# Attention-and-experts kernel, prologue: K's second weights as one doubled transfer, two moved groups of splits, projection weights split in batch 0

## What is computed

```python
h = layernorm(x)                                   # (32, 112, 256)
q = (h @ Wq), k, v = ctx @ Wkv                     # 16 heads of 64
out = softmax(q k^T / 8) v                         # per head, 112 x 375
x = x + out @ Wproj + bproj
h = layernorm(x)
x = x + top-2-of-8 experts(h)                      # silu(h G) * (h U) @ D
```

## Time and profile before

| | |
|---|---|
| median of 3 runs | 1570.44 us |
| the profiled execution | 1568.5 us |
| its span, first to last instruction | 1566.4 us |
| TensorE matmul busy | 1503.0 us (96%) |
| VectorE, ScalarE, GpSimd busy | 968.7, 762.3, 555.2 us |

### The profile page before, as it was taken

How to read it: one execution, slowest core, us unless ns; L and a number is a source line. 1 busy time by engine, 2 the same in 40 slices (tenths; PEclk the granted TensorE clock), 3 DMA queues, 4 the chain that set the end, 5 groups by cost and what they waited for, 6 DMA issues and landing times. The chain is left out here.

```text
span 1566.4 us, 37570 instructions
## 1 busy us (share of the span) xinstructions
PE 1503.0 (96%) x12134; PEld 1321.0 (84%) x12135; DVE 968.7 (62%) x2579; ACT 762.3 (49%) x2091; POOL 555.2 (35%) x636
## 2 busy tenths in 40 slices
PE   4999999999999999999999999999996699999997
PEld 4888888898888888888888888898875588888886
DVE  5667677676766676767767676667675633333332
ACT  3555555555555555555555555555553322222221
POOL 5224233333433243423334343324355122323232
PEclk9999999999999999999999999999997799999999
DMA  5411111111112221111111111221016233332332
GB/s 152 131 50 50 56 49 55 49 55 50 54 54 60 64 73 54 49 54 49 54 49 57 49 54 54 65 69 52 12 66 227 52 52 51 50 54 47 53 50 28
DMA packets 82704, 96.19 MB, mean 61 GB/s; under 512 B 6912, under 2 KB 77808, under 8 KB 82672
## 3 DMA queue, kind: packets, MB, share of 16 engines
q1 hardware_dynamic: 68960, 74.67, 16.5%
q0 software_dynamic: 12144, 15.66, 6.2%
q10 hardware_dynamic: 1568, 5.44, 1.0%
HBM read 44.85 MB, written 50.90 MB: 61 GB/s over the span
## 5 line engine op out<-in xcount | busy, mean ns | idle before, releaser
L767 ACT ACTIVATE prob<-bank,neg_max 112x375 f32<-112x375 f32 x512 | 295.3, 586 | 138.1 <-DVE neg_max L1017 138.1
L1017 DVE TENSOR_REDUCE neg_max<-bank 112x1 f32<-112x375 f32 x512 | 243.9, 539 | 19.4 <-PE bank L1247 19.3
L1257 PE MATMUL bank<-ident,prob 112*125 112x112 f32 x1536 | 214.7, 274 | 2.6 <-ACT prob L767 2.4
L1257 PEld LDWEIGHTS bank<-ident,prob 112*125 112x125 f32 x1536 | 195.9, 188 | 13.8 <-ACT prob L767 4.9
L706 POOL DMA_INDIRECT out<-y_out,dest_now x63 | 97.8, 1552 | 244.1 <-ACT y_out L859 215.0
L895 DVE TENSOR_TENSOR K_l<-bank,K_h 128x376 fp32r<-128x376 f32 x256 | 140.4, 550 | 64.9 <-ACT K_h L727 62.4
L1281 PE MATMUL bank<-probT,V 125*64 125x112 f32 x3072 | 176.6, 264 | 2.0 <-DVE probT L1023 1.1
L1155 PE MATMUL bank<-Wgu,hT_h 128*128 x504 | 175.1, 429 | 2.9 <-DVE hT_l L1112 2.9
L1281 PEld LDWEIGHTS bank<-probT,V 125*64 125x64 f32 x3072 | 149.1, 137 | 14.6 <-issue 2.6
L885 DVE COPY V<-bank 125x512 f32<-125x512 f32 x96 | 66.4, 692 | 151.3 <-PE bank L1219 147.4
L1133 DVE COPY hidT<-bank 128x512 f32<-128x512 f32 x63 | 43.6, 692 | 173.7 <-PE bank L1462 173.7
(11 more groups left out here) (171 smaller groups left out, 3719.9 us busy)
## 6 DMA issues: line engine op xcount, KB each, us to landing
bins<-pad_rows SPq DMA_DIRECT2D x29, 1032.0 KB, 6.2
h_in<-bins SPq DMA_DIRECT2D x63, 129.0 KB, 2.2
y_sb<-in_ctx SPq DMA_DIRECT2D x32, 187.5 KB, 2.4
y_sb<-in_ctx SPq DMA_DIRECT2D x62, 93.8 KB, 2.5
Wgu<-in_L_ffn_gate_up_w SPq DMA_DIRECT2D x4, 1024.0 KB, 5.2
Wgu<-in_L_ffn_gate_up_w ACTq DMA_DIRECT2D x4, 1024.0 KB, 13.2
x_sb<-in_x SPq DMA_DIRECT2D x16, 224.0 KB, 2.8
x_res<-in_x SPq DMA_DIRECT2D x32, 112.0 KB, 5.6
```

Of the source, the lines that this page charges most:

```text
L767: nc.scalar.activation(prob[:, j, :], S_ps[j][0:LQ, 0:LKV], ACT.Exp, bias=neg_max[:, j:j + 1], accum_out=row_sum[:, head // HB, head % HB: ...
L1017: nc.vector.tensor_reduce(neg_max[:, j:j + 1], S_ps[j][0:LQ, 0:LKV], AX.X, ALU.max, negate=True).then_inc(max_done, 1)
L1257: last = nc.tensor.transpose(S_ps[j][0:KR, t * LQ:t * LQ + LQ], prob[:, j, t * KR:t * KR + KR], ident[0:LQ, 0:LQ])
```

## The change

Four edits:

1. `load_tail` fetches the 64 rows in one transfer whose source names them twice (an outermost dimension of 2 with stride 0, then 64 rows of 4 KB), instead of two transfers of 64 rows; its semaphore counts 16 instead of 32.
2. On ScalarE's queue K's tail is issued ahead of the context's tail, and V's tail behind the wait for the context.
3. ScalarE evacuates K4, K5, q2 ahead of `WvH` and `WvT`; VectorE makes the low parts of K4, K5, q2, K6 ahead of `WvL` and `WvU`.
4. The projection weights are no longer split by GpSimd. ScalarE makes `WpH` at the end of step 1 of batch 0, VectorE makes `WpL` at the end of step 3 of batch 0.

```diff
         def load_tail(eng, w, cols, landed):
 
-            eng.dma_start(w[0:CT, :], Wkv[P:CTX, cols]).then_inc(landed, 16)
-            eng.dma_start(w[CT:P, :], Wkv[P:CTX, cols]).then_inc(landed, 16)
+            eng.dma_start(w[:], Wkv[P:CTX, cols].unsqueeze(0).to_broadcast([2, CT, HD])).then_inc(landed, 16)
...
             split_y(1, 1, None)
-
-            wp_hi, wp_lo = (t[:].rearrange("p k n -> p (k n)") for t in (WpH, WpL))
-            pool.wait_ge(wp_in, 16)
-            pool.tensor_copy(wp_hi, wp[:].rearrange("p k n -> p (k n)")).then_inc(wp_done, 1)
-            pool.wait_ge(wp_done, 1)
-            pool.tensor_tensor(wp_lo, wp[:].rearrange("p k n -> p (k n)"), wp_hi.bitcast(F32), ALU.subtract).then_inc(wp_done, 1)
...
             a = Ahead(None)
+            load_tail(act, wk_tail, k_cols, wk_tail_in)
             load_context_tail(act, 0, 0)
-            load_tail(act, wk_tail, k_cols, wk_tail_in)
+            act.wait_ge(y_in[0], 48)
             load_tail(act, wv_tail, v_cols, wv_tail_in)
-            act.wait_ge(y_in[0], 48)
             nc.scalar.copy(yA_h[:, 0, 0:LKV], y_sb[:, 0, 0, :]).then_inc(y_hi, 1)
...
-            for k in range(a.find(1, "K", 4)):
+            for k in range(a.find(1, "K", 6)):
                 evacuate(a, k)
             act.wait_ge(wv_in, 16)
             hi_of_weight(WvH[:], wv[:])
-            act.wait_ge(wv_tail_in, 32)
+            act.wait_ge(wv_tail_in, 16)
             hi_of_weight(WvT[:], wv_tail[:])
-            for k in range(a.find(1, "K", 4), len(a.items)):
+            for k in range(a.find(1, "K", 6), len(a.items)):
...
                         for k in made_at["V"][:1]:
                             evacuate(a, k)
+                        if known(b) and b == 0 and s == 1:
+                            act.wait_ge(wp_in, 16)
+                            nc.scalar.copy(WpH[:].rearrange("p k n -> p (k n)"),
+                                           wp[:].rearrange("p k n -> p (k n)")).then_inc(wp_done, 1)
...
-            for k in range(a.find(1, "K", 1), a.find(1, "K", 4)):
+            for k in range(a.find(1, "K", 1), a.find(1, "K", 7)):
                 low_part(a, k)
             low_of_weight(4, WvL[:], wv[:], WvH[:])
             low_of_weight(5, WvU[:], wv_tail[:], WvT[:])
-            for k in range(a.find(1, "K", 4), len(a.items)):
+            for k in range(a.find(1, "K", 7), len(a.items)):
                 low_part(a, k)
...
                         for k in made_at["V"][1:]:
                             low_part(a, k)
+                        if known(b) and b == 0 and s == 3:
+                            dve.wait_ge(wp_done, 1)
+                            nc.vector.tensor_tensor(WpL[:].rearrange("p k n -> p (k n)"), wp[:].rearrange("p k n -> p (k n)"),
+                                                    WpH[:].rearrange("p k n -> p (k n)").bitcast(F32),
+                                                    ALU.subtract).then_inc(wp_done, 1)
```

More of the change, by code:

```diff
@@ L748, in _ @@
             hi_of_weight(WkH[:], wk[:])
-            act.wait_ge(wk_tail_in, 32)
+            act.wait_ge(wk_tail_in, 16)
             hi_of_weight(WkT[:], wk_tail[:])
```

## The result

The changed kernel takes 1586.92 us (median of 4 runs, 1586.01 to 1587.16) against 1570.71 us before; the ratio is 1.0106, with an interval of 1.0092 to 1.0119: slower by 16.2 us. The forecast was 1589.3 with a range of 1571 to 1597.

The account below looks back on a forecast made before the run. TensorE, busy 96% of the span, was taken as the bound, so its stalls add one for one. Prologue shift (T - 8.8) - 1.4 plus body 0.7 + 1.4 gave +18.9: 1570.44 to 1589.3 us, range 1571 to 1597.

Parts of the forecast that it names:

- The doubled transfer on two engines: Prologue loads: the transfer is cut along its outermost dimension of 2, so two engines carry 64 rows each; chance 0.80.
- two ends: Cut of the doubled transfer: over 16 engines, context whole at 8.5 us, or over two engines, at 13.5 to 33.
- T = 27: Prologue: T is the moment the context is whole, 6.69 us before the change, forecast at 27 us.
- T + 6.9 to the first product: Prologue: TensorE's first product starts 6.9 us after the context is whole, instead of at 14.46 us.
- T + 12.8 to the first q product: Prologue: first q product starts 12.8 us after the context is whole, against 21.63 us before.
- Q + 9.7 to V: Prologue: V products start 9.7 us after the first q product (Q), 11.8 before, with TensorE idle 2.6 us ahead.
- Q + 15.9 to the first scores: Prologue: first scores 15.9 us after the first q product against 17.3, a gain of 1.4, with the clock falling again.
- 0.7 and 1.4 in the body: Batches 0 and 1: the new splits `WpH` on ScalarE and `WpL` on VectorE delay transposes by 0.7 and 1.4 us.
- The sum: Whole kernel: (T - 8.8) - 1.4 + 0.7 + 1.4 = T - 8.1, which is +18.9 us with T = 27.
- The rival that the transfer is spread: Prologue loads: the doubled transfer is spread like any other, T = 8.5, +0.5 us, 1571 us; chance 0.15.
- The faster rival: Prologue and body: the 4 us wait goes, the clock stays up, new splits fall in slack, 1566 us; chance 0.05.
- the late V tail: Prologue: V's tail on the same two engines lands behind T + 18.1, adding up to 5 us, 1597 us; chance 0.04.

Follow-up runs that it names:

- 16 copies: Changed kernel with each tail fetched as 16 copies of its first 8 rows instead of 2 copies of 64: 1569.99 us, ratio 1.0009 to the kernel before.
- V's tail ahead of the wait: Changed kernel with tails as two 64-row transfers and V's tail issued before the wait for the context: 1569.72 us, ratio 1.0003 to the kernel before.
- halves: Changed kernel with edit 1 undone, K's and V's tails again as two transfers of 64 rows each: 1571.81 us, ratio 1.0023 to the kernel before.
- 4 copies: Changed kernel with each tail fetched as 4 copies of its first 32 rows instead of 2 copies of 64: 1581.64 us, ratio 1.0081 to the kernel before.
- Edits 3 and 4: Kernel before plus edits 3 and 4 only, with loads and their order as before: 1570.42 us, ratio 0.9990 to the kernel before.
- the doubled transfer alone: Kernel before with edit 1 only, both tails as doubled transfers in the old order behind the context's tail: 1581.62 us, ratio 1.0086.
- edit 4: Kernel before plus edit 4 only, ScalarE and VectorE splitting the projection weights in batch 0: 1566.95 us, ratio 0.9968 to the kernel before.
- GpSimd held back: Kernel before with one added wait, so GpSimd splits the projection weights only after VectorE made V's low parts: 1565.88 us, ratio 0.9960.

## Why the prediction was right, point by point

- **The doubled transfer on two engines.** Right: 2.03 engines busy, and the cure by 16 copies. The prediction had chosen it between two ends that no row decided; the experiments on the count now do. The Trainium skill had it in the page DMA: Bandwidth & Descriptors (Why a DMA increments its semaphore by 16 and not by 1), down to the zero-stride case (Rules for kernel authors). The runs agree: 2.03 engines for 2 copies, packets held back on two and on four engines of sixteen for 2 and 4, and 5.5 us from issue to landing for 16.
- **T = 27.** It was 25.25. The fast rate was right (25.6 GB/s for an engine alone, 24.9 in the estimate); how the two queues share an engine was an estimate and came out 1.8 us high.
- **T + 6.9 to the first product**, with the table load behind the wait: 7.0 measured, and the run with V's tail ahead of the wait shows that the position costs some 2 us.
- **T + 12.8 to the first q product.** Wrong by 2.3: it was T + 15.1. `xn` and the xT evacuations ran 1.1 later than summed (`WqL` starts at T + 11.6), and `WqL` took 3.33 where I had put 2.28: GpSimd's split of batch 1's context ran beside it until 38.0. I had seen that GpSimd stops `WvU`, and didn't ask which other wide VectorE operation the shift would bring beside it. The same 3.33 us stands in the runs with halves and with 16 and 4 copies.

  But `WqL` is not what the first q product was short of: TensorE worked on K1 to K3 right up to it. The last of their products starts at 40.09 and the next could start 0.17 later, at 40.26; `WqL` ends at 40.16. By these rows a `WqL` of 2.28 us would have gained 0.05. With 16 and with 4 copies the first q product starts 0.46 and 0.47 us behind the end of `WqL`, where it is 0.15 before and after, so there the K products alone held it. They are the term that the sum had put at nothing: 15 products that begin only behind `xn`, at 35.78, and last 4.5 us. Twelve of them took 0.52 us or more, as products of this width do at a granted clock of 0.51 (before, in the window from 1175 us; row below), the last one 0.34. The clock column says 1.00 there, so the lower level is my reading of the durations.

```profile
1180.67 0.52 PE L1247 MATMUL bank<-K_h,q_h 64*112 64x376 f32 x2
```

  T was 1.8 too high and this step 2.3 too short, so they nearly cancelled: the right total is in part luck.

- **Q + 9.7 to V, Q + 15.9 to the first scores.** Measured 9.5 and 15.9. The wait moved from q4 to V as forecast (2.48 us against 2.6), and behind it the granted clock was 0.51. The steps to V hold two slips that nearly cancel: the terms listed up to K6's high part add up to Q + 7.5, not 7.0, and q2's high part was made at Q + 4.35, not 4.9. Edits 3 and 4 together gain 1.8 us in the first scores of their own run (38.97 to 37.16), of which 0.4 lies ahead of the first q product (21.24 against 21.63); from there it is the 1.4 of the sum.
- **0.7 and 1.4 in the body.** 0.6 and 1.6.
- **The sum.** Forecast +18.9, measured +16.2 by the medians, +17.8 in the span, 19.4 in the timeline at batch 1. The shift of the prologue was not the same in the profile and in the medians, as the sum had taken it to be; the 1.9 us by which the profile of before is faster than its median account for a part of that.
- **The rival that the transfer is spread** was put at T = 8.5 and +0.5 us. With the cut undone it was T = 10.6 (9.7 with 16 copies) and +3.3 us (+1.5). The step that failed there is the landing of the context's tail behind K's tail, taken from bytes over a mean rate and 0.7 that no row gave; and T + 12.8 was too short there as well (it was T + 15.8 with halves, where two issues stand ahead of the table load). With halves the change would have been slower by 0.23%.
- **The faster rival and the late V tail** did not come: the clock fell behind the wait, the new splits showed (0.6 and 1.6), and `WvT` had no wait for V's tail in the changed kernel. With the doubled transfer alone that wait was there, 1.59 us.

## What to carry to other kernels

Put a row count that 16 divides outermost in a transfer: a copy count of 2 in front took 512 KB from 5 to over 20 us, and all that queued behind it. Of two engines that disturb each other, hold back the one whose result isn't due (one wait, 6.0 us) before moving its work onto the path. And when waits are moved, look at what the wait was attached to: here a table load of 1.28 us slid behind it.

## What the runs showed of the hardware that I had not expected

- An engine that serves both queues is late with the small share: with its rows of K's tail halved (4 copies against 2) T fell by only 5 us, from 25.3 to 20.3. How it divides its time between the queues isn't settled by these runs.
- Behind TensorE's 2.48 us of idling ahead of V the granted clock fell to 0.50, in the changed kernel, with halves, with 16 and 4 copies, with V's tail ahead of the wait, and with edits 3 and 4; behind the 1.1 to 1.6 us ahead of the first q product it stayed at 1.00, before and in the runs with edits 3 and 4, edit 4, and GpSimd held back.
- The first transfer with 2 or 4 copies took longer to issue on ScalarE's queue, 1.17 and 1.18 us (1.09 in the old order), against 0.66 with 16 copies and 0.57 for 64 rows. V's tail, in the same form, took 0.57, 0.59 and 0.54 us: the form alone is not the cause, and what is stays open.
